# A convolution-attention-experts kernel: the last block but one attended a unit sooner, the first slots turned between logits and counts, token rows loaded in three parts

## What is computed

```python
x = _L0_conv_ref(x, ...)                  # 8 heads, each token looks at its 7x7 neighbours; projected, gated, layer norm
t = _to_tokens(x)                         # (2, 1024, 128)

# additive attention over the 1024 tokens of an image, 32 hidden units
n = _ln_t(t)
q, k = n @ Wt, n @ Wx
h = tanh(q[:, :, None, :] + k[:, None, :, :] + bh)
a = softmax(h @ Wa[:, 0] + ba, axis=-1)
t = t + a @ n

# 8 experts of 128 -> 512 -> 128; each token goes to its best one, each expert takes at most 320
n = _ln_t(t)
probs = softmax(n @ gate_w + gate_b)
idx = argmax(probs);  pos = place of the token among those of its expert;  kept = pos < 320
buf[idx, pos] = n
y = relu(buf @ w1 + b1) @ w2 + b2
t = t + y[idx, pos] * (probs[idx] * kept)
```

## Time and profile before

| what | value |
|---|---|
| median of 3 runs | 666.19 us (665.96 to 670.08) |
| the profiled execution | 666.21 us; its span is 664.4 us |
| PE busy | 536.7 us (81%), 4545 instructions |
| ACT busy | 578.8 us (87%) |
| DVE busy | 486.2 us (73%) |
| POOL busy | 487.1 us (73%) |
| mean granted clock of PE | 0.964 |

### The profile page before, as it was taken

One profiled execution on the slowest core, in us unless ns is written; L12 is line 12 of the kernel. 1 busy time (PEld: TensorE's weight loads), 2 busy tenths in 40 slices (PEclk: granted clock), 3 DMA queues, 4 the chain that ended last, 5 costly groups with the idle time before them and its releaser, 6 DMA issues.

```text
span 664.4 us, 12448 instructions
## 1 busy us (share of the span) xinstructions
PE 536.7 (81%) x4545; PEld 266.3 (40%) x4545; DVE 486.2 (73%) x1372; ACT 578.8 (87%) x417; POOL 487.1 (73%) x585
## 2 busy tenths in 40 slices
PE   9999879998989889986967966676686667776993
PEld 6666533343444334443323312222231222336872
DVE  3767677879888877786678897877868787833455
ACT  3777599999999999999999999999999999960540
POOL 1004688988979768979989997979888797911474
PEclk9999998999999989999879999989989999997997
DMA  9700100100000000005300000000000000003300
GB/s 317 239 1 2 65 1 5 61 1 5 10 5 10 5 0 14 11 5 204 162 0 13 9 5 13 1 14 9 4 9 5 13 0 14 7 4 100 81 27 28
DMA packets 14236, 24.65 MB, mean 37 GB/s; under 512 B 1296, under 2 KB 11058, under 8 KB 13152
## 3 DMA queue, kind: packets, MB, share of 16 engines
q1 hardware_dynamic: 12768, 20.96, 9.2%
q0 software_dynamic: 1408, 2.91, 1.3%
HBM read 17.12 MB, written 7.37 MB: 37 GB/s over the span
## 4 chain that ended last, share of the span: by engine, by line
PE 32%; issue 22%; ACT 21%; DVE 18%; POOL 5%; DVEq 0%; POOLq 0%; ACTq 0%
ACT front L1268 18%; PE ps L967 7%; DVE front L1562 3%; PE ps L1148 3%; PE ps L758 3%; POOL front L628 3%; PE ps L806 2%; PE ps L1152 2%; PE ps L787 2%; PE ps L1004 2%; DVE back L1377 2%; DVE back L1404 1%; PE ps L797 1%; POOL x_one L605 1%; PE ps L873 1%
## 5 line engine op out<-in xcount | busy, mean ns | idle before, releaser
L628 POOL TENSOR_SCALAR front<-k,q 128x1024 f32<-128x1024 f32 (+1 forms) x424 | 388.1, 934 | 43.8 <-PE ps L967 36.3
L1268 ACT ACTIVATE front<-front 128x4096 f32<-128x4096 f32 (+1 forms) x125 | 418.7, 3398 | 1.4 <-POOL front L628 0.8
L967 PE MATMUL ps<-front,cst 128*32 128x512 f32 x2032 | 254.2, 621 | 72.6 <-ACT front L1268 65.6
L1562 DVE TENSOR_SCALAR front<-ps,q 128x512 f32<-128x512 f32 x218 | 188.3, 902 | 19.8 <-PE ps L967 16.5
L967 PEld LDWEIGHTS ps<-front,cst 128*32 128x32 f32 x2032 | 55.3, 112 | 188.2 <-issue 97.6
L1194 ACT ACTIVATE back<-back,mn 128x320 f32<-128x320 f32 (+1 forms) x128 | 62.7, 542 | 9.6 <-DVE mn L1377 9.6
L1377 DVE CUSTOM_DVE_ANT_0 back<-ps,back 128x320 f32<-128x320 f32 (+1 forms) x128 | 54.0, 469 | 10.3 <-PE ps L758 8.9
L1594 DVE COPY ptm<-ps 128x512 f32<-128x512 f32 x31 | 21.4, 692 | 37.6 <-PE ps L993 35.9
L1256 ACT ACTIVATE front<-k,q 128x1024 f32<-128x1024 f32 (+1 forms) x50 | 46.2, 956 | 2.1 <-DVE k L1673 2.1
L575 POOL TENSOR_TENSOR lnw<-lny,lnh 128x4 f32<-128x4 f32 (+1 forms) x9 | 1.8, 200 | 57.7 <-DVEq L1537 52.4
L758 PE MATMUL ps<-conv 32*128 32x320 f32 (+1 forms) x256 | 38.4, 472 | 1.6 <-DVE mn L1377 1.3
(11 more groups left out here) (164 smaller groups left out, 673.1 us busy)
## 6 DMA issues: line engine op xcount, KB each, us to landing
back<-in_w SPq DMA_DIRECT2D x2, 2048.0 KB, 11.0
xbuf<-rec SPq DMA_DIRECT2D x1, 2720.0 KB, 21.8
back<-in_top SPq DMA_DIRECT2D x2, 1024.0 KB, 5.8
back<-in_bottom SPq DMA_DIRECT2D x2, 1024.0 KB, 9.0
front<-xbuf SPq DMA_DIRECT2D x2, 720.0 KB, 6.7
back<-in_inner SPq DMA_DIRECT2D x1, 1280.0 KB, 9.9
back<-in_b SPq DMA_DIRECT2D x1, 1280.0 KB, 15.9
xT<-in_xT SPq DMA_DIRECT2D x4, 256.0 KB, 5.8
```

What stands on the lines that cost most here:

```text
L628: last = nc.gpsimd.tensor_scalar(ring[u % DEPTH][:, at + lo:at + hi], k4[:, img * L + k0 + lo:img * L + k0 + hi], q4[:, m:m + 1], 1.0, ALU ...
L967: last = nc.tensor.matmul(bank(to)[c * U:(c + 1) * U, :], c_("wa", U - QPG - QPG * row, 2 * U - QPG - QPG * row), ring[t % DEPTH][:, at:at ...
L1268: last = nc.scalar.activation(ring[t % DEPTH][:, 0:to], ring[t % DEPTH][:, 0:to], ACT.Tanh)
L1562: last = nc.vector.tensor_scalar(ring[u % DEPTH][:, at + lo:at + keys], ps[:, base + k0 + lo:base + k0 + keys], q4[:, m:m + 1], None, ALU.add)
```

## The change

There are three edits.

1. `phase_step`: block 14's phases below 8 stand two steps sooner than the rule (before: one), those from 8 on three steps sooner (before: two). Each phase of block 14 moves up one unit.
2. The turning of the first five tiles of slots leaves `place_slots` and becomes `turn_first_slots`, which PE does in the last block's step between `logits` and `counts`, with its wait for `ld_xe[0]`. The 6 products of `keep_clock(6, 3)` that stood behind it are gone.
3. `xr` is fetched in three parts (tiles 0-5, 5-10, 10-20) in place of two. `gate_exps` and `weights` go by these parts: ACT does `gate_exps(0)` ahead of the copies of the next slots, and DVE does `weights(1)` behind expert 0's output and `weights(2)` behind expert 1's. `weighted_bias` and `send` on POOL wait accordingly.

```diff
+PARTS = ((0, 5), (5, 10), (10, TILES))
 def phase_step(p, phase):
-    return PEND[p] + 1 + phase - (0 if p != NB - 2 else 1 if phase < 8 else 2)
+    return PEND[p] + 1 + phase - (0 if p != NB - 2 else 2 if phase < 8 else 3)
...
             fetch(xe, 5, 10, 0, C, ld_xe[1])
-            fetch(xr, 0, 10, C, REC, ld_xr[0])
+            fetch(xr, 0, 5, C, REC, ld_xr[0])
+            fetch(xr, 5, 10, C, REC, ld_xr[1])
             fetch(xe, 10, TILES, 0, C, ld_xe[2])
-            fetch(xr, 10, TILES, C, REC, ld_xr[1])
+            fetch(xr, 10, TILES, C, REC, ld_xr[2])
...
             def weighted_bias(q):
-                pool.wait_ge(prb_ready, 1 + q // 2)
+                pool.wait_ge(prb_ready, min(q, 2) + 1)
...
-                if k in (0, 10):
-                    pool.wait_ge(dest_ready, 1 + k // 10)
+                if k in (0, 5, 10):
+                    pool.wait_ge(dest_ready, 1 + k // 5)
...
+            def turn_first_slots():
+
+                pe.wait_ge(ld_xe[0], 16)
+                for k in range(PLACED):
+                    nc.tensor.matmul(bank(4 + k // 3, k % 3 * P, (k % 3 + 1) * P), xe[:, k, :], c_("ident"),
+                                     start=(k % 3 == 0), stop=False)
...
                 if p is not None:
                     logits(t, p)
+                if p == NB - 1:
+                    turn_first_slots()
                 p = query_block(t, 10)
...
             def place_slots():
 
-                pe.wait_ge(ld_xe[0], 16)
-                for k in range(PLACED):
-                    nc.tensor.matmul(bank(4 + k // 3, k % 3 * P, (k % 3 + 1) * P), xe[:, k, :], c_("ident"),
-                                     start=(k % 3 == 0), stop=False)
-                keep_clock(6, 3)
                 pe.wait_ge(xn_ready, NB)
...
-            def gate_exps(half):
-                act.wait_ge(ld_xr[half], 16)
+            def gate_exps(i):
+                lo, hi = PARTS[i]
+                act.wait_ge(ld_xr[i], 16)
...
                     rectified(e + 1)
+                if e == 0:
+                    gate_exps(0)
                 if e % 2 == 0 and e + 2 < NE:
                     turned_slots(e // 2 + 1)
                 if e < 2:
-                    gate_exps(e)
+                    gate_exps(e + 1)
...
             for e in range(NE):
                 slots_out(e)
-                if e == 0:
-                    weights(1)
+                if e < 2:
+                    weights(e + 1)
```

More of the change, by code:

```diff
@@ L443, in program @@
         centred, place_ready, ld_count = sem("centred"), sem("place_ready"), sem("ld_count")
-        ld_xe, ld_xr = [sem(f"ld_xe{i}") for i in range(3)], [sem(f"ld_xr{i}") for i in range(2)]
+        ld_xe, ld_xr = [sem(f"ld_xe{i}") for i in range(3)], [sem(f"ld_xr{i}") for i in range(3)]
         xeT_done, xeT_ready = sem("xeT_done"), sem("xeT_ready")
@@ L1324, in rectified @@
                                          bias=c_("b1", e * FC + c, e * FC + c + 1)).then_inc(h_out, 1)
-            def gate_exps(half):
-                act.wait_ge(ld_xr[half], 16)
-                nc.scalar.activation(lge[:, half * 10:(half + 1) * 10, :], xr[:, half * 10:(half + 1) * 10, C:C + NE],
-                                     ACT.Exp).then_inc(ge_ready, 1)
+            def gate_exps(i):
+                lo, hi = PARTS[i]
+                act.wait_ge(ld_xr[i], 16)
+                nc.scalar.activation(lge[:, lo:hi, :], xr[:, lo:hi, C:C + NE], ACT.Exp).then_inc(ge_ready, 1)
             turned_slots(0)
@@ L1807, in _, with weights @@
                     dve.sem_inc(t_ready[3], 1)
-            def weights(half):
-                lo, hi = half * 10, (half + 1) * 10
-                dve.wait_ge(ld_xr[half], 16)
+            def weights(i):
+                lo, hi = PARTS[i]
+                dve.wait_ge(ld_xr[i], 16)
                 nc.vector.tensor_copy(dest[:, lo:hi], xr[:, lo:hi, C + NE]).then_inc(dest_ready, 1)
-                dve.wait_ge(ge_ready, half + 1)
+                dve.wait_ge(ge_ready, i + 1)
                 link(nc.vector.tensor_reduce(zg[:, lo:hi], lge[:, lo:hi, :], AX, ALU.add))
```

## The result

The changed kernel takes 663.75 us (median of 22 runs, 661.45 to 670.87), the kernel before 667.46 us beside it (22 runs, 665.29 to 670.08). The ratio is 0.995 with a 95% interval of 0.9937 to 0.9963: a gain of 3.3 us, between 2.5 and 4.2, which lies within the one per cent that was forecast. (The two medians lie 3.7 us apart.) Timed once more beside the kernel before, the same kernel measured 0.9962 (0.9944 to 0.998), a gain of 2.5 us. The forecast was 4.3 us.

What follows compares the result with a forecast made beforehand. ACT sets the pace up to 587 us, then a ladder with one engine at work at a time, then PE bounds the experts. Sum: 666.2 - 1.0 - 4.8 - 0.2 + 1.7 = 661.9 us; range 659.5 to 664.2.

Steps and rivals of the forecast that it cites:

- the rival of PE held at the first slots: First slots' fetch lands late and delays block 15's `counts`: 663.6 us, spread over 663 to 665; chance 0.10.
- The copy a rung sooner: DVE's copy of block 15's first turned half no longer waits for block 14's `slotted`: 1.0 us gained, bounds 0.8 and 1.2.
- The 0.2 us by which the last energies should slip: PE does block 14's `counts` instead of `logits` just ahead of the last energies, which come 0.2 us later.
- The price upstream: ACT softens block 14 straight behind unit 120; DVE's minimum is ready 0.15 us before needed, so costed at nothing.
- The hold, costed at nothing: PE's `turn_normed` of block 14 waits for `normed`, starting unit 125's energies about 1 us late; costed at nothing.
- Turning and keeping out from behind `slotted`: Between block 15's `slotted` and the placing, PE no longer turns first slots or runs keeping products: 4.8 us gained.
- The first slots hidden: Fetch lands in 3.2 us and turning takes 1.24 us, between PE's `logits` and `counts`, with 0.2 us to spare.
- The clock: PE's clock falls after its pauses, slowing placing and first products: 1.7 us charged, bounds 0 and 3.4; forecast case 0.62.
- The 0.2 us for placing at full clock: Without a fall, placing and first products run at full clock, saving 0.2 us of placing's slow stretch.
- No fall, the rival: PE's clock stays up over placing and first products: 660.2 us, range 659.8 to 660.6; chance 0.20.
- The third edit at nothing: Fetching `xr` in three parts: waits on ACT and later sends on POOL are hidden; costed at 0.

Runs made afterwards that it cites:

- both pauses filled: Changed kernel plus ten products that only keep PE working, four ahead of the wait for the first slots, six behind block 15's `counts`: 661.37 us, ratio 0.9913.
- `normed` sooner: Changed kernel with the ten keeping products, plus DVE's part of block 14's `normed` put ahead of unit 127's sums: 661.05 us, ratio 0.9913.
- the second pause alone: Changed kernel plus six keeping products behind block 15's `counts`, none ahead of the wait for the first slots: 659.61 us, ratio 0.9906.
- the two-part fetch: Changed kernel with the ten keeping products, but token rows fetched in two parts as before: 660.91 us, ratio 0.9933.

## Why the prediction was right, and where a term was off

The time lies in the range, but the mechanism that the forecast named would have put it at 661 to 663. That 663.75 falls where the prediction had the rival of PE held at the first slots (663 to 665) is no sign of that rival: the rows of both traces show the fall of the clock, and `counts` as long after the copy as before.

**The copy a rung sooner: right.** 1.0 us was forecast, with DVE's copy following PE's turning; the traces have 1.10 (2.77 against 3.87 us). The 0.2 us by which the last energies should slip didn't come: they end 1.96 us after the last tanh in thirteen of the fourteen traces. Their last products follow ACT's last piece, and a later start leaves them only less to wait for.

**The price upstream: right.** ACT had 0.24 us to spare at block 14's softening (0.15 forecast) and no gap.

**The hold, costed at nothing: right as a rule, but with little to spare, and with an exception.** It was 0.97 to 0.98 us in six traces that have the first edit, and there was no loss there. But PE stands idle for some 2.25 us at the hold, and in five of these six the clock was at its lower level for 3.4 us straight behind it. Rows of the changed kernel's second trace:

```profile
584.50:587.90 3.40, 3.40 (x22) 1.04 (x18) 0.76 (x5) 3.40 (x3) 0.00 (x0) 0.50 0.00 0
```

```profile
589.47 0.37 PE L1028 MATMUL ps<-osum,ones 128*128 128x8 f32 x2
```

Block 14's `counts` so ended at 589.84, 0.08 us ahead of the last tanh (589.92); in the one trace of the six without this fall they ended 1.3 us ahead of it. The prediction had the late start, but not that the pause would slow what follows. In the first profiled execution the clock was at its lower level from 572.0 to 578.8 while block 14 was turned; unit 125's energies started 2.99 us late, and the last energies ended 1.84 us later than otherwise. How often this comes is open; taking the hold away changed no median by more than the intervals can tell.

**Turning and keeping out from behind `slotted`: right.** 4.8 forecast, 4.83 measured.

**The first slots hidden: right at full clock.** The landing took 2.94 us (3.2 assumed) and the turning 1.38 (1.24 assumed), and `counts` came as late after the copy as before (8.56 us). The margin of 0.28 us is as thin as forecast. It is used up not by a late landing, as the rival had it, but when the fall begins at the turning (1.04 us in two kernels).

**The clock: the mechanism was right, the size wrong.** This is the term that was mis-sized. The step charged 1.7 us, 0.24 of a stretch of 7.0 us in the middle of the units. In that stretch the kernel before was at the lower level for only 3.3 us or a little more:

```profile
431.90:435.20 3.30, 3.30 (x16) 0.92 (x12) 0.63 (x2) 3.30 (x2) 2.15 (x3) 0.50 0.13 42
```

Here the fall lasted twice as long or more in five traces (6.8 to 10.2 us) and lay over all of the placing and most of the first products, work that is all in the ladder. These five have 8.21 to 8.77 us for placing and first products; without a fall it is 6.04. So such a fall costs 2.2 to 2.7 us, between the value taken and the upper bound of 3.4. The first profiled execution had a short one (3.5 us), which cost 1.1 us, less than the charge (7.14 against 6.04). The 0.2 us for placing at full clock were 0.13 (6.17 to 6.04). With these sizes the sum is -1.1 - 4.8 - 0.1 + 2.2 to 2.7, that is a gain of 3.3 to 3.8 us, against 3.3 and 2.5 us by the two timings of the changed kernel and the 4.3 forecast. The first profiled execution lost its part elsewhere: 1.84 us at the last energies, 0.97 us in placing and first products against before, and 0.5 us behind them, so that 2.6 us of gain were left after the last tanh (71.25 against 73.83).

The Trainium skill, "TensorE: Matmul & The Clock Gate", section "HAM oscillation — how this bites in real kernels", has the wait that follows each short burst of products as what sends the clock down. The traces agree as to the cause, since bursts with pauses of 1.1 and 2.0 us had the fall and it was gone where both were filled; the waits of the page's example are longer, some 3 to 5 us, and here the shorter ones were enough.

**No fall, the rival:** 660.2 us was worked out for it. The kernel with both pauses filled, which has ten more products, is the nearest to it that was run: 0.9913 of the 666.2 us on which the sum rests is 660.4.

**The third edit at nothing:** no run shows a difference, alone or on top of the others, though the intervals leave room for one to two microseconds.

**The level.** The sum stood on an execution of 666.2 us; the kernel before ran at 666.67 to 667.46 in the comparisons. Of the 1.85 us between 661.9 and 663.75, 1.3 are this level (667.46 against 666.2); the rest is the gain, which by medians was 3.7 for 4.3.

## What to carry to other kernels

When work is taken out from in front of a wait, ask what its engine does in the pause that is left: here about half of the 4.8 us removed came back as a lower clock over the next products in most traces. Price such a fall by the work that lies under it in the chain, at both levels of the clock, not by a mean over a stretch elsewhere. Look at all the pauses around the critical products: with only one of two filled, the clock still fell in the execution that was profiled. And take the filling at the lower clock when asking whether it fits into its pause: six products of 2.9 us did not fit into 2.0.

The best version found is the changed kernel with both pauses filled, 0.9913 of the time before (0.9889 to 0.9936), 5.8 us. That with `normed` sooner as well (0.9913), the second pause alone (0.9906) and the two-part fetch (0.9933) can't be told apart from it by their intervals; of these it is the one whose runs lie closest together.

## What the runs showed of the hardware that was not expected

Two executions of the same code differ by 2.3 us before the change begins. The changed kernel's unit 120 ended at 566.34 in one and at 564.05 in the other. They part between 305 and 368 us. The stretch from 332 to 348 us in the two (the execution that lost time first):

```profile
332.00:348.00 16.00, 11.56 (x63) 4.45 (x67) 10.85 (x41) 14.25 (x9) 12.09 (x15) 0.57 0.00 1
```

```profile
332.00:348.00 16.00, 10.94 (x77) 3.98 (x81) 11.75 (x43) 15.56 (x10) 13.99 (x17) 0.89 0.00 1
```

The same code was granted 0.57 there in one and 0.89 in the other, and ACT was busy 14.25 and 15.56 of the 16 us. Most of this came between 343 and 348 us; that the clock caused it isn't shown. The last tanh falls into two groups over all fourteen traces, 589.9 to 590.6 and 591.4 to 592.7, whatever the kernel, so a single profile can't be read against another one's clock time to better than about 2 us.

The same number of keeping products held the clock in one kernel and not in another: with the turning between them they did, and with 1.68 us of idle time left they did not.
